# Norm and routing chains in small pieces between the row maxima, and the projections' store and GpSimd subtraction later in their queues

## What is computed

```python
h = _layernorm(x) * (1 + ca) + sa                       # norm 1
q, k, v = lora_linear(h, ...)                            # q, k: exact to float32 by three bf16 parts
attn = softmax(where(causal, q @ k.T / 4, -inf))         # row maximum, exponential, sum
x = x + ga * lora_linear(attn @ v, wo, ao, bo)
h = _layernorm(x) * (1 + cb) + sb                       # norm 2
scores = softmax(h @ Wg.T + bg); topv, topi = top_k(scores, 2)
h_e = relu(h @ Wi.T + (h @ A[e].T) @ B[e].T)             # for each expert e
x = x + gb * sum_e w_e * (h_e @ Wo.T)
```

## Time and profile before

| | us |
|---|---|
| median of 3 runs | 2129.84 (2129.48 to 2133.99) |
| profiled execution, own time | 2129.05 |
| its span, first to last instruction | 2127.3 |
| PE busy | 1889.3 (89%) |
| DVE busy | 1219.6 (57%) |
| ACT busy | 943.9 (44%) |
| POOL busy | 489.7 (23%) |
| mean granted PE clock | 0.957 of 2.4 GHz |

### The profile page before, as it was taken

How to read it: one execution, slowest core, us unless ns; L and a number is a source line. 1 busy time by engine, 2 the same in 40 slices (tenths; PEclk the granted TensorE clock), 3 DMA queues, 4 the chain that set the end, 5 groups by cost and what they waited for, 6 DMA issues and landing times.

```text
span 2127.3 us, 31511 instructions
## 1 busy us (share of the span) xinstructions
PE 1889.3 (89%) x11124; PEld 978.3 (46%) x11124; DVE 1219.6 (57%) x2729; ACT 943.9 (44%) x1701; POOL 489.7 (23%) x791
## 2 busy tenths in 40 slices
PE   7699887999889997999979999799988999799858
PEld 5233443545335453454534454354533545343535
DVE  3767585555755566555665558555575555654142
ACT  2256553454444544444444444345444454444321
POOL 3122112222122312222122221222212231122213
PEclk9899998999899998999999999999989999899979
DMA  5413221212201122021211212121220112110100
GB/s 169 84 51 72 71 69 45 68 33 66 80 10 61 31 66 80 16 70 33 68 60 34 68 30 71 45 68 34 65 80 8 63 31 66 31 38 3 36 0 20
DMA packets 103024, 111.37 MB, mean 52 GB/s; under 512 B 20084, under 2 KB 96976, under 8 KB 102872
## 3 DMA queue, kind: packets, MB, share of 16 engines
q1 hardware_dynamic: 102856, 109.34, 18.1%
q10 hardware_dynamic: 16, 0.02, 0.0%
HBM read 75.20 MB, written 33.57 MB: 51 GB/s over the span
## 4 chain that ended last, share of the span: by engine, by line
PE 72%; DVE 14%; ACT 6%; issue 4%; SPq 2%; DMA 2%; POOL 1%; ACTq 0%; POOLq 0%; DVEq 0%
PE ov L768 11%; PE dense L848 11%; PE st L753 10%; PE mxs L739 10%; PE dense L859 5%; PE dense L825 5%; PE dense L783 5%; PE dense L833 4%; DVE negm L1139 3%; PE dense L724 3%; ACT probs L907 2%; PE mxs L743 2%; SPq L580 1%; PE dense L850 1%; DVE negm_left L1139 1%
## 5 line engine op out<-in xcount | busy, mean ns | idle before, releaser
L907 ACT ACTIVATE probs<-st 128x512 f32<-128x512 f32 (+1 forms) x1216 | 669.2, 575 | 653.8 <-PE st L753 644.1
L1139 DVE TENSOR_REDUCE negm<-mxs 128x1 f32<-128x384 f32 (+4 forms) x736 | 427.0, 615 | 212.7 <-PE mxs L743 209.6
L739 PE MATMUL mxs<-k_st,q_st 96*128 96x512 bf16 (+3 forms) x1536 | 469.7, 333 | 65.6 <-DVE negm L1139 59.4
L753 PE MATMUL st<-q_st,k_st 98*128 98x512 bf16 (+3 forms) x1536 | 452.8, 334 | 56.6 <-DMA q_st<-m_row 40.8
L1139 DVE TENSOR_REDUCE negm_left<-mxs 128x1 f32<-128x512 f32 x512 | 335.3, 685 | 139.8 <-PE mxs L739 138.7
L768 PE MATMUL ov<-probs,v_g 128*32 128x512 f32 (+3 forms) x3072 | 331.2, 501 | 19.5 <-POOL probs L633 18.7
L739 PEld LDWEIGHTS mxs<-k_st,q_st 96*128 96x128 bf16 x1536 | 149.4, 98 | 333.2 <-DVE negm L1139 181.6
L848 PE MATMUL dense<-c_t,wi_t 128*128 128x512 f32 x512 | 246.8, 604 | 3.9 <-ACT ratio_b L957 3.7
L753 PEld LDWEIGHTS st<-q_st,k_st 98*128 98x128 bf16 x1536 | 139.3, 99 | 240.4 <-ACT probs L907 92.4
L646 POOL TENSOR_TENSOR hid<-hid,second 128x512 f32<-128x512 f32 x128 | 159.7, 1270 | 294.1 <-DVE second L1207 293.5
L630 POOL TENSOR_TENSOR fence<-fence 128x1 f32<-128x1 f32 x256 | 49.9, 195 | 668.0 <-ACT probs L907 667.8
(11 more groups left out here) (162 smaller groups left out, 1680.8 us busy)
## 6 DMA issues: line engine op xcount, KB each, us to landing
q_st<-q_parts_scratch SPq DMA_DIRECT2D x384, 64.0 KB, 2.8
k_st<-k_parts_scratch SPq DMA_DIRECT2D x384, 64.0 KB, 2.9
q_parts_scratch<-q_part SPq DMA_DIRECT2D x16, 768.0 KB, 3.3
k_parts_scratch<-k_part SPq DMA_DIRECT2D x16, 768.0 KB, 4.9
xin<-in_L_attn_x SPq DMA_DIRECT2D x9, 1024.0 KB, 5.5
x<-in_L_attn_x SPq DMA_DIRECT2D x8, 1024.0 KB, 5.6
out_x<-ob SPq DMA_DIRECT2D x64, 128.0 KB, 1.7
q_st<-m_row SPq DMA_DIRECT2D x128, 4.0 KB
```

Of the source, the lines that this page charges most:

```text
L739: last = nc.tensor.matmul(mxs[:, bank_m, j * n:(j + 1) * n], q_st[0:KS, slot, h0 + j, qt * P:(qt + 1) * P], k_st[0:KS, slot, h0 + j, k0:k0 ...
L753: last = nc.tensor.matmul(st[:, score_bank(ch, kt, h0), j * n:(j + 1) * n], k_st[0:KS + 2, slot, h0 + j, kt * P:(kt + 1) * P], q_st[0:KS + ...
L907: nc.scalar.activation(probs[:, par, h0:h0 + heads, 0:n], st[:, score_bank(ch, kt, h0), 0:heads * n].rearrange("p (j q) -> p j q", q=n), A ...
L1139: nc.vector.tensor_reduce(dst[:, h0:h0 + heads], src, axis=AX.X, op=ALU.max, negate=True).then_inc(max_free, 1)
```

## The change

1. Both norms are cut into 4 pieces of statistics (2 tiles each) and 7 of `ln`: the aggregations with 3 links, one Newton step, two Newton steps, four pieces with 2 scalings each. Routing is cut into 6 pieces of 6, 4, 5, 1, 3 and 6 operations. The operations are the same.
2. These pieces are no longer fillers. `norm_steps` gives each a unit, and each unit's pieces are spread among its other steps: norm 1 over u0 to u3, norm 2 over u6 to u9, routing over u12 to u14.
3. What depends on them moves: `t1` from unit 3 to 5, the first projections from 4 to 6 (five of them, before four), `mt` and `rb` from 14 to 15.
4. `ps` of the first half stands one projection later, and SP waits for one POOL subtraction fewer than the plan has by then.
5. POOL also holds its part of a projection back, until it has run the next `qk` step (with its mask, if it has one) or a step on which POOL has work.

```diff
     early = [("pj", w, ot, half) for ot in range(2) for half in range(2) for w in "qk"]
-    early.insert(4, ("ps", 0))
+    early.insert(5, ("ps", 0, 1))
...
-        put(0, ("ls1",))
...
-        put(1, ("ln1",))
...
-        put(3, *[("t1", i) for i in range(4)], ("xin",))
-        put(4, *early[:5])
+        put(5, *[("t1", i) for i in range(4)], ("xin",))
+        put(6, *early[:6])
+        put(11, *early[6:7])
     if post:
-        put(9, ("ls2",), ("ln2",))
-    if pre:
-        put(11, *early[5:7])
-    if post:
-        put(11, *[("t2", i) for i in range(4)], ("rt",), ("rx",), ("ro",))
+        put(11, *[("t2", i) for i in range(4)], ("rt",), ("rx",))
...
-        put(14, *[("mt", v) for v in range(2)], *[("rb", half) for half in range(2)])
+        put(15, *[("mt", v) for v in range(2)], *[("rb", half) for half in range(2)])
...
+    chains = []
+    if pre:
+        chains += norm_steps("1", 0)
+    if post:
+        chains += norm_steps("2", 6) + [(12 + i // 2, ("ro", i)) for i in range(ROUTE_PARTS)]
...
+        beside = [s for at, s in chains if at == u]
...
+        turns += [((i + 0.6) / len(beside), 3, s) for i, s in enumerate(beside)]
...
+POOL_IDLE = frozenset("mx pv qk nm ce ov vg ms rs t1 t2 ls1 ls2 ln1 ln2 ro ct op rt rx".split())
+STAT_PARTS = 4
+NORM_PARTS = 7
+ROUTE_PARTS = 6
+def norm_steps(which, first):
+    steps = [("ls" + which, i) for i in range(STAT_PARTS)] + [("ln" + which, i) for i in range(NORM_PARTS)]
+    return [(first + (i + 1) // 3, s) for i, s in enumerate(steps)]
...
-            if held_back and s[0] not in ("mx", "pv", "qk"):
+            if held_back and s[0] not in passes:
                 run(*held_back.pop())
...
-                if held_back and s[0] == "mx":
+                if held_back and s[0] == until:
                     run(*held_back.pop())
...
-                    ot = a[0]
-                    sp.wait_ge(part3_ready, done("pj"))
+                    ot, later = a
+                    sp.wait_ge(part3_ready, done("pj") - later)
...
-            walk(pool, NB, run)
+            walk(pool, NB, run, late="pj", passes=POOL_IDLE, until="qk")
...
-            walk(dve, NB, run, late="pj")
+            walk(dve, NB, run, late="pj", passes=("mx", "pv", "qk"), until="mx")
```

More of the change, by code:

```diff
@@ L220, in relus_covered, with chain_steps @@
     return steps
+POOL_IDLE = frozenset("mx pv qk nm ce ov vg ms rs t1 t2 ls1 ls2 ln1 ln2 ro ct op rt rx".split())
[5 more added lines that the diff above has]
+    return [(first + (i + 1) // 3, s) for i, s in enumerate(steps)]
+def chain_steps(names):
+    parts = {"ls": STAT_PARTS, "ln": NORM_PARTS, "ro": ROUTE_PARTS}
+    return [(n, i) for n in names for i in range(parts[n[:2]])]
 def hidden_quads(half):
@@ L233, in prologue_plan @@
     plan = [("su", i) for i in range(N_PROJECTION_SETUP)]
-    plan += [("ls1",), ("ln1",)] + [("t1", i) for i in range(4)] + [("xin",)]
-    plan += pj[0] + [("ps", 0)] + [("rs", g, half, g) for g in range(2) for half in range(2)]
+    plan += chain_steps(("ls1", "ln1")) + [("t1", i) for i in range(4)] + [("xin",)]
+    plan += pj[0] + [("ps", 0, 0)] + [("rs", g, half, g) for g in range(2) for half in range(2)]
     plan += [("vp", i) for i in range(4)] + [("vg", 0)]
@@ L274, in tallied @@
         names.append("qk diagonal")
+    if step[0] in ("ln1", "ln2") and step[1] == NORM_PARTS - 1:
+        names.append("normed")
+    if step[0] in ("ls1", "ls2") and step[1] == STAT_PARTS - 1:
+        names.append(step[0] + " all")
+    if step == ("ro", ROUTE_PARTS - 1):
+        names.append("routed")
     if step[0] == "rs":
@@ L297, in with_banks, with walk @@
     return steps, n % 2
-def walk(eng, batches, run, late=None):
+def walk(eng, batches, run, late=None, passes=(), until=None):
     counts = {}
@@ L324, in phase @@
                 counts[n] = counts.get(n, 0) + 1
+        assert not held_back
     phase(prologue_plan(), -1)
@@ L1035, in normalise, with route @@
                                                         op1=ALU.mult))
[L1036 to L1043 removed]
+                if i == 0:
+                    dve.wait_ge(norm_chain, links + T)
+                    nc.vector.memset(fence[:, 3:4], 0.0)
+                    for t in range(T):
+                        nc.vector.bn_aggr(mv[:, t, :], stats[:, t, :]).then_inc(norm_chain, 1)
+                    dve.wait_ge(norm_chain, links + 2 * T)
+                    link(nc.vector.tensor_scalar_add(var, mv[:, :, 1], LN_EPS))
+                    link(nc.vector.tensor_scalar(b.bitcast(I32), var.bitcast(I32), 1, None, ALU.arith_shift_right))
+                    link(nc.vector.tensor_scalar(y.bitcast(I32), b.bitcast(I32), -1.0, RSQRT_SEED, ALU.mult, ALU.add))
+                elif i == 1:
+                    newton()
+                elif i == 2:
+                    k[0] = 2 * T + 6
+                    newton()
+                    newton()
+                    assert k[0] == NORM_LINKS
+                else:
+                    for t in range(2 * i - 6, 2 * i - 4):
+                        last = nc.vector.tensor_scalar(dst[:, t, :], src[:, t, :], mv[:, t, 0:1], y[:, t:t + 1],
+                                                       ALU.subtract, ALU.mult)
+                    if i == NORM_PARTS - 1:
+                        last.then_inc(ready, 1)
+            def route(n, i):
+                at = (0, 5, 9, 14, 15, 18)[i]
+                k = [at]
                 def link(ins):
```

178 lines of the change are left out of this document (88 added, 90 removed).

## The result

The changed kernel takes 2137.68 us, median of 20 runs (2135.83 to 2150.83); the kernel before 2131.6, median of 20 beside it. The ratio is 1.0046, 95% interval 1.0031 to 1.006: slower by 0.5%, where 2095 us were forecast. Of the changed kernel's executions 7 took 2148 to 2151 us, at a granted clock of 0.939 to 0.941, and 13 took 2136 to 2139 at 0.946 to 0.950, of which the profile shows one, while of the kernel before one execution of 2751.57 us is left out of the ratio. The profiled execution spans 2135.6 us (2127.3 before), with a mean granted clock of 0.948 (0.957).

What follows compares the result with a forecast made beforehand. PE, busy 89% of the span, was taken as the bound. Terms of 1.4 - 3.3 + 6.5 + 0.8 + 0 = 5.4 us per full body, six bodies 32, together 34 with body 0, gave 2095 us; range 2062 to 2122.

Steps and rivals of the forecast that it cites:

- u0 to u4: Norm 1 in pieces: DVE stays the bound in u0 to u3, 1.9 us saved, 0.5 returned in u4; gain 1.4.
- u5 to u8: Norm 2's pieces ahead of the maxima: DVE 21.3 us plus 2.5 of cast waits, 23.8 against 20.55; loss 3.3.
- u9 to u11: Gap behind u8: 3.1 us gained by the queues, 3.4 by the fifth projection, 0.8 by full clock in u11.
- The projection's 3.4 + 0.8: Fifth projection moved into the gap behind u8 saves 3.4 us; the sixth at full clock in u11 saves 0.8.
- u12 to u15: Routing in pieces: the 4.4 us wait only moves to `mt`; taken as 0, bounds -0.4 to +3.
- Holding back on POOL costs nothing.: POOL's held part of a projection costs nothing, since the store and DVE's projection after next need it much later.
- B at full clock: Stretch u5 to u8 was counted without clock loss, because a similar prologue row showed clock 1.00.
- Rival 3: Clock also falls in u0 to u4 and u5 to u8: 5 us per body, 2125 us; chance 0.05.
- Body 0, body 1 and body 7: Body 0, norm 1 only: 2.5 us gained; body 1 a full body, 5.4; body 7: 0, between -5 and +5.
- Rival 2: Slower, pieces behind projections make DVE wait 2.3 us for casts, four more such waits: +20, 2149 us; chance 0.08.

Runs made afterwards that it cites:

- s1: Kernel before with only norm 1 in pieces over u0 to u3; norm 2, routing and both queues as before: 2126.65 us, ratio 0.9979.
- s8: Changed kernel with the score matmuls issued during u4 and u8 issued three times over, same values into the same bank: 2118.72 us, ratio 0.9949.
- s2: Kernel before with only norm 2 in pieces over u6 to u9: 2154.94 us, ratio 1.0112.
- s9: Changed kernel, but DVE's held part of a projection lets the pieces of norms and routing pass: 2125.09 us, ratio 0.9964.
- s12: Kernel before with only the store put behind the maxima's DMAs on SP's queue: 2112.54 us, ratio 0.9902.
- s4: Kernel before with only the queues changed: store behind the maxima's DMAs, POOL's subtraction held back, fifth projection in the gap behind u8: 2110.8 us, ratio 0.9903.
- s13: Changed kernel with the fifth projection back in u11, the store behind it: 2168.24 us, ratio 1.016.
- s3: Kernel before with only routing in pieces over u12 to u14 and `mt` behind u14: 2139.6 us, ratio 1.0036.
- s10: Changed kernel with POOL's subtraction issued at once, as before; the store stays behind the maxima's DMAs: 2130.05 us, ratio 0.9988.
- s16: s11 with POOL's subtraction issued at once, as in the kernel before: 2086.4 us, ratio 0.9785.
- s11: Kernel before with norm 1 in pieces, changed queues, norm 2's statistics in u5 and u6, last two projections in u12: 2086.06 us, ratio 0.9778.

## Why the prediction was wrong

- **A sum counted twice.** u0 to u4 were credited with 1.4 us, the leaving transposes in it. For u5 to u8 the forecast 23.8 us were then compared with 18.65 + 1.9, as if these 1.9 us had been gained elsewhere. By its own terms the sum is 1.4 - 5.15 + 6.5 + 0.8 = 3.55 us per body, 2105. This is bookkeeping: compare each stretch's new length with its old one, and let moved work appear once on each side.
- **u0 to u4 (forecast 1.4 gained, measured 2.4).** The bound was another one. DVE was to be it in u0 to u3, for a gain of 1.9 us. There PE is busy 19.29 of 20.05 us, and the stretch is 6.0 us shorter; DVE's backlog is worked off in u4, which takes 3.6 us more (forecast 0.5), at a low clock.
- **u5 to u8 (forecast 23.8, measured 26.7).** The step that failed is taking the longer of two sums over four units: PE 20.3, DVE 21.3 plus casts. The transposes fall into u5 and u6, where PE is the bound (s1: +3.0, about 1.0 of it the clock in u5, by s8), the norm's pieces into u7 and u8, and in u8 DVE is busy 7.55 of 8.00 us (s2: +4.7). The two add up, 18.6 + 7.7 = 26.3. The counted waits for casts were not the cause (s9); forecast at 2.5 us, they were one of 0.64.
- **u9 to u11 (forecast 7.3 less, measured 6.3).** The mechanism was right. s12 gives 2.9 us to the store's order (3.1 forecast). The projection's 3.4 + 0.8 are 2.8 to 5 in the changed kernel, but hang on norm 2 having left (s4, s12, s13). What frees the gap is what costs in u7 and u8.
- **u12 to u15 (forecast 0, bounds -0.4 to +3 gained, measured 2.9 lost).** The wait ahead of `mt`, forecast at 4.4 us, is there (4.1 to 4.7). The step that failed is DVE's sum up to `mt`, forecast at 16.9 us against 16.7 before, 15.15 of it work and 1.7 a wait for a cast. The first `mt` comes 19.6 us after the end of u11 (before, 16.5 to 17.1), 2.9 us later in the mean. In body 2 that is 16.95 us of work and 2.45 idle, 1.06 of it the wait for the cast. The work is 1.8 us more than forecast because the same operations last longer beside POOL's subtractions: L1122 1.16 us instead of 0.19, and a copy, L1130, 1.69 instead of 1.00 (rows in the last section). These two make 1.7 us, a term that the prediction put at nothing; the first comes with the pieces (s3 and s10 have it too), the second with holding the subtraction back (in s10 it is gone). From `mt` to the end of u15 it takes 12.8 us in the mean, as before (12.9): the 1.6 us that u14 took away and the 1.7 us of clock came out even, as forecast, though the clock's price varies, with lengths of 11.6 to 13.6 us for the same work.
- **"Holding back on POOL costs nothing."** It costs 7.6 us with the pieces (s10, 5.9 by the two profiled executions) and nothing where norm 2's second half and routing are whole (s16 and s11). I looked only at who needs the third part, not at what DVE does while POOL computes it.
- **"B at full clock".** Wrong. One row of the prologue, where PE was busy 3.39 of 4 us, stood for u4 and u8, where it is busy 5 of 8: the clock was 0.72 to 0.81 in u4 and 0.68 to 0.81 in u8 over bodies 2 to 6. In u4, and behind it in u5, it costs time (s8: 0.9 and 1.0 us per body); in u8 s8 gained nothing in the mean, since the clock fell there all the same in four bodies of five. Rival 3 had this mechanism and nearly its size, 5 us per body (s8: 4.2), at a chance of 0.05. The Trainium skill's rule that I set aside ("TensorE: Matmul & The Clock Gate", "A second HAM failure mode: psum-queue depth-cycling") says that TensorE's clock goes back and forth where it idles briefly and often between groups of matmuls that cycle through PSUM banks. In u4 the trace agrees, with waits for banks of 1.5 us at most, and s8, 19 us faster, shows that it costs time.
- **Body 0, body 1 and body 7.** Body 0 was forecast to gain 2.5 us and ends 5.7 us earlier (s1: 5.2); body 1 was counted with 5.4 gained and loses 2.3. From body 7 on 0 was forecast, 0.5 lost.

By stretches, in the mean over bodies 2 to 6, after minus before: -2.4 + 8.1 - 6.3 + 2.9 = +2.3 us. With 3.4 gained ahead of body 2 and 0.5 lost from body 7 on that is 5 x 2.3 - 3.4 + 0.5 = +8.6 (the spans differ by 8.3). Rival 2 had the sign and a price of 20 us, but not the cause: it decided "from 2.4 more full waits on", full being 2.3 us, and in body 2 DVE waits for casts 0.64 us in u7, 1.14 and 0.75 in u9, and 1.06 in u13. Slower came from several small causes together: norm 2's pieces in u8, transposes in u5 and u6, the clock, and operations of DVE beside POOL's. Without one of them the time is under that of the kernel before (s8 0.9949, s9 0.9964, s10 0.9988), but still 24 to 35 us over the forecast.

## What to carry to other kernels

Work it out unit by unit, for each engine, and add up the longer ones: the longer of two sums over a stretch hides that the loads lie at different times. A gap that hides an engine's long chain isn't free time; fill it only with work whose chain has another place to go, as norm 2's statistics had in u5 and u6. And where another engine is the bound and TensorE has many short waits, price the stretch and the one behind it with a fallen clock too (here 0.72 to 0.81 in u4). At last, a sum of runs of the parts that meets the total isn't yet a proof: compare them stretch by stretch.

## What the hardware showed that I had not expected

**More work can be faster.** s8's tripled scores made the changed kernel 19 us faster; in u4, where it is shown, by holding the clock.

**The same instructions run at different clocks.** The first 8.5 us of u3 in bodies 2 and 4 of the kernel before, then its first 7.0 us in bodies 2 and 3 of s3; u3 has the same instructions in every body:

```profile
534.50:543.00 8.50, 7.63 (x38) 5.40 (x39) 7.65 (x13) 2.46 (x5) 0.00 (x0) 0.80 0.00 0
...
1039.80:1048.30 8.50, 7.63 (x22) 5.27 (x23) 6.48 (x11) 1.79 (x3) 0.00 (x0) 0.60 0.00 0
```

```profile
535.80:542.80 7.00, 6.11 (x15) 3.93 (x16) 5.51 (x10) 1.19 (x2) 0.00 (x0) 0.51 0.00 0
...
791.90:798.90 7.00, 6.15 (x37) 4.44 (x38) 6.93 (x12) 2.42 (x5) 0.00 (x0) 1.00 0.01 2
```

Clock 0.80 and 0.60, and u0 to u3 last 25.0 and 26.6 us; clock 0.51 and 1.00, and they last 26.5 and 23.5. In s3 the waits of PE just ahead are the same to 0.03 us in both bodies. A body's length carries some 3 us that no instruction explains, so one body is no basis for terms of 1 us.

**POOL stops DVE.** In the changed kernel a DVE operation that lasts 0.19 us alone takes as long as the subtraction beside it. The copy of the routing, first in the kernel before, then in the changed one, is stretched too:

```profile
594.08 1.16 POOL L670 TENSOR_TENSOR q_part<-rest,q_part 128x512 bf16<-128x512 f32 x1 [3.60 <-DVE q_part L1216]
594.12 1.16 DVE L1122 TENSOR_TENSOR rv<-rv,rs_ 128x32 f32<-128x32 f32 x1
```

```profile
594.52 1.00 DVE L1080 COPY second<-rs_ 128x1024 f32<-128x1024 f32 x1
```

```profile
599.94 1.16 POOL L670 TENSOR_TENSOR k_part<-rest,k_part 128x512 bf16<-128x512 f32 x1
599.95 1.69 DVE L1130 COPY second<-rs_ 128x1024 f32<-128x1024 f32 x1
```

The operations of the first pair, L670 and L1122, both read two operands in SBUF. The Trainium skill ("SBUF — State Buffer", "SBUF: two separate sides") says that DVE with two SBUF inputs and GpSimd share ports under an exclusive lock, for the whole instruction. The trace agrees: 1.16 us in each of the six bodies where a subtraction runs beside it, 0.19 in the last two, where none does. Before the change two thirds of the overlap of DVE with POOL's subtractions was with maxima, whose operand is in PSUM; in the changed kernel it is under a third.
